# First attention of a four-layer kernel: where the rows of maxima are turned, and pairs of scores in the last waves

## The chip, the cores and the metric

The kernel runs as one program on one core of a Trainium2 chip. The metric is the device time of one execution in microseconds (us), as the median of several runs. The kernel before takes 2932.99 us in the median of 3 runs (2932.86 to 2940.77).

The engines are named as in the profile: PE (TensorE, matrix products and transposes), PEld (its weight loads), DVE (VectorE), ACT (ScalarE), POOL (GpSimd) and SP (the engine that issues the DMAs). PE writes its products into eight banks of PSUM (`P[:, 0]` to `P[:, 7]`), each 512 float32 wide on 128 partitions. Every engine runs its own list of instructions in order, and semaphores tie the lists together.

## What is computed

```python
x = L0_attn_x                                   # (4, 1024, 128)
x = x + attention(layernorm(x))                 # 16 heads of 8, inner layer norm, softmax, own residual
x = x + experts(layernorm(x))                   # a shared and 8 routed experts, top 2
x = x + differential_attention(layernorm(x))    # 8 heads, two softmaxes of 128 each
x = x + fp4_ffn(layernorm(x))                   # blockwise quantized
```

The change touches the first attention alone. For every batch and head it is

```python
scores = einsum('bhqd,bhkd->bhqk', q, k) / sqrt(8)
attn   = softmax(scores, axis=-1)
out    = einsum('bhqk,bhkd->bhqd', attn, v)
```

## The kernel before, in words

**Units and waves.** The first attention is cut into 16 units `u` (4 batches, 4 groups of four heads each). `plan_all` writes one order of steps by hand; each engine then walks through that order and takes the steps it has a part in. A stage `s` has 8 slots `i`. In every slot there is one `maxima` step of unit `u`, one `scores` step of a unit that lies `LAG0` = 7 stages back, and in slots 1 and 5 a `sums` step of one stage further back. What lies between two `sums` steps, four slots, is called a wave here. Unit `u` starts at stage `8u`.

**maxima (L1633 on PE, L1216 on DVE).** Queries times keys of one head `j` (32 of the array's rows) into one bank, 128x512; DVE reduces it to a row maximum. The four heads use four different row groups of the array. Banks: the ring 0, 1, 2, 3.

**row1, row2, row2_low.** When a unit has half of its maxima, `row1` (L1223, DVE) folds them into 16 columns, `row2` turns them with one PE transpose (L1639), ACT copies the result twice (L773, L774), POOL takes the rest (L2001), and SP issues eight small DMAs (L2097) that write the maxima into two rows of `a_Qs`. The `scores` of that half wait for these DMAs. The SP step also waits for all `maxima` that stand before it in the plan.

**scores (L1645 on PE, L780 on ACT).** Keys times queries of one head into one bank of the ring 5, 6, 7; ACT takes the exponential into `a_PT`. A wave has four of them.

**sums (L1660 on PE).** Probabilities times values, four heads in four column groups, 8 instructions, accumulated in bank 4. After eight of them ACT copies the bank to `a_OT` (L788).

**divide (L1668 on PE, L1230 and L1234 on DVE).** Four transposes of `a_OT`, then the division by the sums. Banks: the ring 0 to 3.

**Order around the change.** Slot 0: maxima of head 0, scores of head 2; slot 1: heads 1 and 3, then `sums`; slot 2: heads 2 and 0; slot 3: heads 3 and 1; slots 4 to 7 likewise. Further steps are hooked on behind a slot. `row2` of unit `u` stands behind slot 3 of stages `8u+4` and `8u+8`, and `divide` of unit `u-1` behind slot 4 of the same stages.

**The last waves.** From stage 128 on no maxima are left; the scores of unit 15 from its third wave on, and its sums, run with only the first steps of the experts beside them: statistics and normalization, `m_turn_x` (L1692), `route` (L1702, 24 small products), `choose`, `spread` (L1708), and `turn_o` (L1675) and `out_project` (L1683) of the last batch. After the last `sums` and the last `divide` the first expert item (L1721) starts.

Of the kernel before, what the change touches and what calls it, by code (L numbers as in the profile page):

```python
# [8 lines left out]
ACT = mybir.ActivationFunctionType  # L9
# [9 lines left out]
SCALE = float(8.0 ** -0.5)  # L19
NU = 4 * B  # L20
LAG0 = 7
NE, NI = 9, 256
LAG = 3
NITEM = 2 * B * 2 * NE
# [7 lines left out]

class Ctx:
    pass


class Once:
# [46 lines left out]
class Tally:  # L84
# [15 lines left out]
    def at(self, name, *step, i=None):  # L100

        return name, self.value[name, step] - (0 if i is None else self.by[name, step] - i)
# [44 lines left out]
def snapped(on_dve):  # L147
# [19 lines left out]
    "row2_low": lambda u, c: {"a_mt_low": 1, f"a_mdma{u % 3}_{c}": 128},  # L167
    "maxima": {"a_max_pe": 1, "a_max_dve": 1},
    "scores": {"a_st": 1, "a_exp": 1},
    "sums": lambda u, hs: {"a_pv": 1, "a_oe": 1} if hs % 8 == 7 else {"a_pv": 1},  # L170
    "divide": {"a_ot_pe": 1, "a_rc": 1, "a_on": 1},
    "turn_o": {"a_oc_pe": 1, "a_oc_act": 1},
# [69 lines left out]
    "row2": lambda *a: [("a_mt_act", "row2", *a)],  # L242
    "maxima": lambda *a: [("a_max_dve", "maxima", *a)],
    "scores": lambda *a: [("a_exp", "scores", *a)],
    "sums": lambda u, hs: [("a_oe", "sums", u, 15)],
    "divide": lambda *a: [("a_on", "divide", *a)],
    "turn_o": lambda *a: [("a_oc_act", "turn_o", *a)],
# [29 lines left out]
def plan_all():  # L277

    p = Plan()
    ring = Ring([0, 1, 2, 3])  # L280
    act_ring = Ring([5, 6, 7])

    def on_ring(*step):
        p.on([ring.take()], *step)

    def norm(who, b):
        return ([("ln_stats", who, b, k) for k in range(4)] + [("ln_gather", who, b, k) for k in range(2)] +
                [("ln_apply", who, b, k) for k in range(4)])

    def put(step):  # L290
        if step[0] in RINGED_ACT:
            p.on([act_ring.take()], *step)
        elif step[0] in RINGED:
            on_ring(*step)
        else:
            p.do(*step)
        for slots, s in FOLLOWS.get(step[0], lambda *a: ())(*step[1:]):
            p.later(slots, *s)
# [4 lines left out]
    def hook(s, slot, *step):  # L303
        hooks.setdefault((s + slot // 8, slot % 8), []).append(step)
# [14 lines left out]
    for u in range(NU):  # L319
        b, gr = divmod(u, 4)  # L320
        s0 = 8 * u
        if gr == 1 and b + 1 < B:
            for i, f in enumerate(norm("x", b + 1) + norm("xn", b + 1)):
                hook(s0, 5 * i + 4 * (i // 10), *f)
            for c in range(2):
                hook(s0 + 15 + c, 3, "turn_h", b + 1, c)
                hook(s0 + 19 + c, 7, "values", b + 1, c)
        if u + 1 < NU:
            for w, c in ((1, 0), (1, 1), (0, 0), (0, 1)):
                hook(s0 + 3 - w, 1, "project", u + 1, w, c)  # L330
        for c in range(2):
            hook(s0 + 3 + 4 * c, 7, "row1", u, c)
            hook(s0 + 4 + 4 * c, 3, "row2", u, c)
        e0 = s0 + LAG0
        for r in range(2):
            hook(e0 + 5 + 4 * r, 4, "divide", u, r)
            if gr == 3:
                hook(e0 + 6 + 4 * r, 7, "turn_o", b, r)
                hook(e0 + 7 + 4 * r, 5, "out_project", b, r)
# [14 lines left out]
    ahead = iter(ahead)  # L354
    for s in range(8 * NU + LAG0 + 2):
        for i in range(8):
            um, m = divmod(2 * s + i // 4, 16)
            ue, m_e = divmod(2 * (s - LAG0) + i // 4, 16)
            up, m_p = divmod(2 * (s - LAG0 - 1) + i // 4, 16)
            if um < NU:  # L360
                t, half = (m % 4, m // 4) if um == 0 and m < 8 else (m // 2, m % 2)
                on_ring("maxima", um, t, i % 4, half)
            if 0 <= ue < NU:
                p.on([act_ring.take()], "scores", ue, m_e, (i + 2) % 4)
            if i % 4 == 1 and 0 <= up < NU:
                if m_p == 0:
                    p.on([4], "sums", up, m_p)
                else:
                    p.do("sums", up, m_p)
            for step in hooks.get((s, i), ()):  # L370
                put(step)
            if ue == NU - 1:
                for step in next(ahead, ()):
                    put(step)
            p.tick()
# [15 lines left out]
    for b in range(1, B):  # L391
        m = 36 * (b - 1)
# [5 lines left out]
    at = [30, 33, 44, 66, 69, 80, 102, 105]  # L398
# [59 lines left out]
    for j in range(NJ - 1):  # L458
        n = 16 * j + 28.5
        at = {NJ - 3: (0, 1, 1.5, 6, 8, 10, 12, 14, 14.5, 18, 19, 20),  # L460
              NJ - 2: (0, 1, 1.5, 5, 6, 6.5, 7, 7.5)}.get(j, (0, 1, 1.5, 6, 8, 10, 12, 14, 14.5, 19, 20, 32))
# [63 lines left out]
def memory(nc, io):  # L525

    m = Ctx()
    where, top = {}, 16512

    def put(name, shape, dt, offset):  # L530
        t = nc.alloc_sbuf_tensor_at(name, shape, dt, offset=offset)
        where[t.name] = name, shape, offset
        return t

    def sb(name, shape, dt=F32):
        nonlocal top
        t = put(name, shape, dt, top)
        top += (4 * math.prod(shape[1:]) + 31) // 32 * 32
        return t
# [41 lines left out]
    assert top >= A_EARLY + 16384, top  # L581
    m.Ks[0] = sb("a_Ks0", [128, T], F32R)
    m.Qs[0] = sb("a_Qs0", [128, T], F32R)
    m.PT = [[sb(f"a_PT{j}_{i}", [128, 512]) for i in range(4)] for j in range(4)]
    m.Vp = [sb(f"a_Vp{i}", [128, NT * 144 + 32]) for i in range(2)]
    m.tq = [sb(f"a_tq{i}", [128, 512]) for i in range(2)]
    m.th = [sb(f"a_th{i}", [128, 512]) for i in range(2)]
# [117 lines left out]

def a_free(v, *step):

    return [v.at("a_oe", "sums", NU - 1, 7), v.at("a_oe", "sums", NU - 1, 15), v.at("a_st", "scores", NU - 1, 15, 1),
            v.now("a_add", *step), v.now("a_rc", *step)]


def scalar_engine(e, w, v, m):
    at, P = v.at, m.P8

    def bank(*step):
        return P[:, v.plan.bank[step], :]
# [59 lines left out]
    def scores(u, hs, j):  # L776
        w.wait_ge(*at("a_st", "scores", u, hs, j))
        if 16 * u + hs > 3:
            w.wait_ge(*at("a_pv", "sums", *divmod(16 * u + hs - 4, 16)))
        e.activation(m.PT[j][hs % 4][:, :], bank("scores", u, hs, j), ACT.Exp, scale=SCALE).then_inc(m.S["a_exp"])  # L780

    def sums(u, hs):
        c, kt = divmod(hs, 8)
# [32 lines left out]
    def item(n):  # L816
        w.wait_ge(*at("b_gate", "item", n))
        if n > 2:
            w.wait_ge(*at("b_hf", "product", n - 3))
        for t in a_free(v, "item", 0):  # L820
            w.wait_ge(*t)
        e.activation(m.sg[n % 3][:, :], bank("item", n), ACT.Silu).then_inc(m.S["b_sg"])  # L822
# [178 lines left out]
    def l_gate(i):  # L1001
# [1 line left out]
        w.wait_ge(*at("d_h_pe", "d_turn_h", NJ - 2, 1))  # L1003
        tanh(bank("l_gate", i), i)

    parts = dict(first=first, first_hn=first_hn, turn_h=turn_h, project=project, row2=row2, scores=scores, sums=sums,
                 turn_o=turn_o, m_turn_x=m_turn_x, choose=choose, spread=spread, item=item, halves=halves, down=down,
                 small_exp=small_exp, small2=small2, fold=fold, c_turn_x=c_turn_x, keep_x=keep_x,
                 c_project=c_project, exponent=exponent, turn=turn, pv=pv, output=output, weigh=weigh,
# [576 lines left out]
def tensor_engine(e, w, v, m):  # L1586
    at, P, ident = v.at, m.P8, m.ident

    def bank(*step):

        for t in v.freed(*step):
            w.wait_ge(*t)
        return P[:, v.plan.bank[step], :]
# [47 lines left out]
    def scores(u, hs, j):  # L1641
# [3 lines left out]
        e.matmul(ps, m.Ks[u % 3][r, 128 * kt:128 * kt + 128], m.Qs[u % 3][r, 512 * c:512 * c + 512],  # L1645
                 start=True, stop=True).then_inc(m.S["a_st"])

    def sums(u, hs):
        b, gr = divmod(u, 4)
        c, kt = divmod(hs, 8)  # L1650
        O = P[:, 4, :]
        for j in range(4):
            at_v = 144 * kt + 9 * (4 * gr + j)
            w.wait_ge(*at("a_exp", "scores", u, hs, j))
            w.wait_ge(*at("a_v_dve", "values", b, 1))
            if c:
                w.wait_ge(*at("a_oe", "sums", u, 7))
            elif u:
                w.wait_ge(*at("a_oe", "sums", u - 1, 15))
            tt = e.matmul(O[32 * j:32 * j + 32, :], m.Vp[b % 2][:, at_v:at_v + 32], m.PT[j][hs % 4][:, :],  # L1660
                          start=(kt == 0), stop=(kt == 7))
        tt.then_inc(m.S["a_pv"])

# [241 lines left out]
    def l_down(i):  # L1905
# [1 line left out]
        w.wait_ge(*at("d_hT", "d_turn_h", NJ - 1, i))  # L1907
        down_rows(ps[:, 0:128], i).then_inc(m.S["d_dn"])

    parts = dict(turn_h=turn_h, values=values, project=project, maxima=maxima, row2=row2, scores=scores, sums=sums,  # L1910
                 divide=divide, turn_o=turn_o, out_project=out_project, m_turn_x=m_turn_x, route=route, spread=spread,
                 item=item, down=down, finish=finish, small2=small2, fold=fold, c_turn_x=c_turn_x,
                 c_project=c_project, score=score, turn=turn, pv=pv, output=output, turn_weights=turn_weights,
# [272 lines left out]
def build(nc, io, out):  # L2186
    with ExitStack() as ctx:
        v = Tally(plan_all(), SIGNALS, READ)
        m = memory(nc, io)
        m.P8 = ctx.enter_context(nc.psum_tensor("P", [128, 8, 512], F32))  # L2190
        names = ["id", "mh", "a_w", "b_w", *[f"x{b}" for b in range(B + 1)], *v.end]
        m.S = {n: ctx.enter_context(nc.semaphore(n)) for n in dict.fromkeys(names)}
        block = ctx.enter_context(nc.Block())
        block.sync(lambda e: sync_engine(e, Once(e, m.S), v, m, io, out))
        block.scalar(lambda e: scalar_engine(e, Once(e, m.S), v, m))
        block.vector(lambda e: vector_engine(e, Once(e, m.S), v, m))
        block.gpsimd(lambda e: gpsimd_engine(e, Once(e, m.S), v, m))
        block.tensor(lambda e: tensor_engine(e, Once(e, m.S), v, m))
# [66 lines left out]
```

## Time and profile before

| | |
|---|---|
| median of 3 runs | 2932.99 us |
| profiled execution, its own time | 2927.33 us |
| its span | 2925.5 us |
| PE busy | 2744.2 us (94%) |
| DVE busy | 2307.5 us (79%) |
| ACT busy | 2100.6 us (72%) |
| POOL busy | 1802.3 us (62%) |
| first attention in full waves (73.28 to 805.31 us) | 240 waves |
| its last 16 sums without maxima | 805.31 to 861.8 us |

The profiled execution is one run; 1.8 us of its time lie outside the span. Busy shares are means over stages that have different limits, so the stages are read one by one. A matmul of 0.49 us that starts at the same time as its neighbours runs beside them in another row group: the starts tell the pace, not the durations. PEclk is the TensorE clock that the chip granted: 1.00 is 2.4 GHz, 0.50 is 1.2 GHz. A time in square brackets is idle time of the engine ahead of an instruction, with what ended it.

### The profile page before, as it was taken

What the parts mean: (1) busy time and instruction counts of PE and PEld (TensorE: products, weight loads), DVE (VectorE), ACT (ScalarE), POOL (GpSimd) and SP (SyncE); (2) the same over time, 40 slices, a digit from 0 to 9 for tenths busy, and PEclk for the clock granted to TensorE, in tenths of its full rate; (3) what the DMA queues carried; (4) which work ended last, traced back from release to release, by engine and by line L of the source; (5) the groups of instructions that cost most, each with busy time, mean ns of one, the idle gap of its engine ahead of it and who ended that gap; (6) DMA issues with size and microseconds to landing.
All of it is one profiled execution on the core that took longest, in us unless ns stands there. A gap on an engine that the chain in (4) does not pass through costs nothing.

```text
span 2925.5 us, 46589 instructions
## 1 busy us (share of the span) xinstructions
PE 2744.2 (94%) x16447; PEld 2037.2 (70%) x16447; DVE 2307.5 (79%) x4143; ACT 2100.6 (72%) x4692; POOL 1802.3 (62%) x1357
## 2 busy tenths in 40 slices
PE   6999999999899999999999999999999999999996
PEld 3333333333347777788888888888888888888885
DVE  8888888888937887778788777788777877777776
ACT  2777777777755555677777777777777777787773
POOL 3432534332115555677788778788778787777873
PEclk9999999999979999999999999999999999999997
DMA  1000000000021121000000000000000000000000
GB/s 41 7 7 7 12 7 7 7 7 2 2 76 53 47 73 59 8 1 1 1 1 3 1 3 3 3 1 3 3 1 3 3 1 3 3 1 3 3 3 6
DMA packets 25689, 34.83 MB, mean 12 GB/s; under 512 B 4136, under 2 KB 14952, under 8 KB 25456
## 3 DMA queue, kind: packets, MB, share of 16 engines
q1 hardware_dynamic: 25456, 31.85, 3.5%
q8 instruction: 131, 2.15, 0.3%
q14 instruction: 102, 0.84, 0.1%
HBM read 29.08 MB, written 2.23 MB: 11 GB/s over the span
## 4 chain that ended last, share of the span: by engine, by line
PE 69%; DVE 10%; ACT 10%; POOL 5%; issue 5%; DMA 0%; DVEq 0%; POOLq 0%
PE P L1792 17%; PE P L1817 11%; PE P L1660 9%; PE P L1645 5%; PE P L1721 5%; PE P L1803 5%; PE P L1633 4%; ACT a_PT L780 4%; PE P L1826 3%; PE P L1732 3%; PE P L1775 2%; PE P L1623 2%; DVE c_nm L1371 2%; ACT c_P L904 2%; POOL d_tn L1094 2%
## 5 line engine op out<-in xcount | busy, mean ns | idle before, releaser
L1371 DVE TENSOR_REDUCE c_nm<-P 128x1 f32<-128x1024 f32 x512 | 623.8, 1218 | 169.3 <-PE P L1792 169.1
L1216 DVE TENSOR_REDUCE a_mx<-P 128x1 f32<-128x512 f32 x1024 | 640.1, 683 | 94.9 <-PE P L1633 91.6
L904 ACT ACTIVATE c_P<-P,c_nm 128x1024 f32<-128x1024 f32 x512 | 576.0, 1125 | 131.6 <-DVE c_nm L1371 131.4
L780 ACT ACTIVATE a_PT<-P 128x512 f32<-128x512 f32 x1024 | 537.2, 602 | 165.5 <-PE P L1645 165.1
L2039 POOL TENSOR_TENSOR c_P<-c_P,c_P 128x1024 f32<-128x1024 f32 (+1 forms) x256 | 623.2, 2434 | 21.4
L2037 POOL TENSOR_SCALAR c_P<-c_P,c_rr 128x1024 f32<-128x1024 f32 (+1 forms) x256 | 304.4, 1189 | 305.0 <-DVE c_rr L1383 304.9
L1792 PE MATMUL P<-c_xth,c_Th 128*128 128x512 f32 x1024 | 365.8, 438 | 42.8 <-ACT c_P L904 42.6
L1645 PE MATMUL P<-a_Qs,a_Ks 32*128 32x512 f32 x1024 | 343.0, 491 | 59.1 <-ACT a_PT L780 52.6
L1817 PE MATMUL P<-c_DT,c_xkh 128*128 128x256 f32 x2048 | 392.0, 284 | 5.6 <-DVE c_xkl L1363 5.0
L1396 DVE TENSOR_TENSOR c_DT<-P,c_DT 128x512 fp32r<-128x512 f32 x512 | 348.6, 681 | 12.9 <-ACT c_DT L915 12.1
L1817 PEld LDWEIGHTS P<-c_DT,c_xkh 128*128 128x128 f32 x2048 | 330.1, 192 | 6.6 <-DVE c_xkl L1363 5.6
L1792 PE MATMUL P<-c_xtl,c_Th 128*128 128x512 f32 x1024 | 321.4, 395 | 0.0
L1792 PE MATMUL P<-c_xth,c_Tl 128*128 128x512 f32 x1024 | 321.2, 395 | 0.0
L1803 PE MATMUL P<-ident,c_P 128*128 128x128 f32 x2048 | 306.8, 272 | 6.6 <-DVE c_DT L1396 6.5
L915 ACT ACTIVATE c_DT<-P 128x512 fp32r<-128x512 f32 x512 | 309.8, 605 | 1.0 <-PE P L1803 1.0
L1633 PEld LDWEIGHTS P<-a_Ks,a_Qs 32*128 32x128 f32 x1024 | 128.1, 189 | 247.8 <-DVE a_mx L1216 192.1
L2025 POOL TENSOR_TENSOR b_sg<-b_sg,b_cwB 128x512 f32<-128x512 f32 x128 | 176.5, 1382 | 196.8 <-ACT b_sg L822 196.8
L1633 PE MATMUL P<-a_Ks,a_Qs 32*128 32x512 f32 x1024 | 284.2, 494 | 11.3 <-DVE a_Qs L1208 5.4
L1817 PE MATMUL P<-c_DT,c_xkl 128*128 128x256 f32 x1024 | 290.6, 284 | 0.0
L1660 PE MATMUL P<-a_PT,a_Vp 128*32 128x512 f32 x2048 | 280.8, 621 | 0.0
L1803 PEld LDWEIGHTS P<-ident,c_P 128*128 128x128 f32 x2048 | 245.2, 140 | 28.6 <-DVE c_DT L1396 8.0
L1645 PEld LDWEIGHTS P<-a_Qs,a_Ks 32*128 32x128 f32 x1024 | 133.9, 186 | 167.2 <-ACT a_PT L780 141.9
(245 smaller groups left out, 5418.4 us busy)
## 6 DMA issues: line engine op xcount, KB each, us to landing
b_cwB<-cw_scratch SPq DMA_DIRECT2D x64, 256.0 KB, 5.1
c_stg<-in_cw SPq DMA_DIRECT2D x8, 640.0 KB, 3.9
a_Qs<-a_mT SPq DMA_DIRECT2D x256, 2.0 KB
b_stg<-in_moe SPq DMA_DIRECT2D x9, 384.0 KB, 3.1
out<-xres SPq DMA_DIRECT2D x15, 128.0 KB, 1.8
xres<-in_x SPq DMA_DIRECT2D x3, 512.0 KB, 7.2
xres<-in_x SPq DMA_DIRECT2D x2, 256.0 KB, 3.1
a_hTl_f<-in_wqk SPq DMA_DIRECT2D x1, 512.0 KB, 3.7
```

Of the source, the lines that this page charges most:

```text
L780: e.activation(m.PT[j][hs % 4][:, :], bank("scores", u, hs, j), ACT.Exp, scale=SCALE).then_inc(m.S["a_exp"])
L904: e.activation(m.P1[s][n % 4][:, :], P[:, k:k + 2, :].rearrange("p c k -> p (c k)"), ACT.Exp, bias=m.nm[:, n % 4, s:s + 1], accum_out=m.sm ...
L1216: e.tensor_reduce(m.mx2[u % 2][:, t // 4, j, t % 4, half:half + 1], bank("maxima", u, t, j, half), AX, ALU.max).then_inc(m.S["a_max_dve"])
L1371: e.tensor_reduce(m.nm[:, n % 4, s:s + 1], P[:, k:k + 2, :].rearrange("p c k -> p (c k)"), AX, ALU.max, negate=True).then_inc(m.S["c_nm"])
L1396: e.tensor_tensor(lo, bank("turn", n, half).rearrange("p (t q) -> p t q", t=4), hi.bitcast(F32), ALU.subtract).then_inc(m.S["c_dl"])
L1633: e.matmul(ps, m.Qs[u % 3][r, 128 * t:128 * t + 128], m.Ks[u % 3][r, 512 * half:512 * half + 512], start=True, stop=True).then_inc(m.S["a_ ...
L1645: e.matmul(ps, m.Ks[u % 3][r, 128 * kt:128 * kt + 128], m.Qs[u % 3][r, 512 * c:512 * c + 512], start=True, stop=True).then_inc(m.S["a_st"])
L1660: tt = e.matmul(O[32 * j:32 * j + 32, :], m.Vp[b % 2][:, at_v:at_v + 32], m.PT[j][hs % 4][:, :], start=(kt == 0), stop=(kt == 7))
L1792: tt = e.matmul(ps[:, c, :], a[:, s, qs], x[:, 512 * c:512 * c + 512], start=(i == 0), stop=(i == 2))
L1803: tt = e.transpose(ps[:, 128 * i:128 * i + 128], m.P1[0][n % 4][:, 128 * kt:128 * kt + 128], ident)
L1817: tt = e.matmul(ps[:, 0:256], x[:, 128 * kt:128 * kt + 128], m.DT[p % 2][l][:, kt, :], start=(kt == 0 and j == 0), stop=(kt, j) == (7, 2))
L2039: e.tensor_tensor(p0, p0, p1, ALU.add).then_inc(m.S["c_D"])
```

## The change

Two things are moved or added, both in the first attention.

1. `row2` is hooked behind slot 5 instead of slot 3 of the same stage. In slot 5 it stands right behind the `sums`. Its followers (`row2_low`, two slots later) move with it.
2. The scores of the last unit from stage 128 on (`hs` 2 to 15) become `pair` steps: two matmuls into two neighbouring banks, (2, 3) for heads 2 and 3 and (5, 6) for heads 0 and 1, with one semaphore increment, and one exponential over both banks (128x1024). For that `a_PT` becomes one tensor. The other steps of that stretch have the rings 0, 1 and 7.

```diff
+SCORE_HEADS = ((2, 3), (0, 1))
+def paired(u, hs):
+    return u == NU - 1 and hs >= 16 - 2 * LAG0
+def scores_of(u, hs, j):
+    return ("pair", u, hs, 1 if j < 2 else 0) if paired(u, hs) else ("scores", u, hs, j)
...
+    score_pairs = Ring([(2, 3), (5, 6)])
...
-            hook(s0 + 4 + 4 * c, 3, "row2", u, c)
+            hook(s0 + 4 + 4 * c, 5, "row2", u, c)
...
+            if um == NU and m == 0 and i == 0:
+                ring.slots, ring.i, act_ring.slots, act_ring.i = [0, 1], 0, [7], 0
+            if 0 <= ue < NU and paired(ue, m_e):
+                if i % 2 == 0:
+                    p.on(score_pairs.take(), "pair", ue, m_e, i % 4 // 2)
+            elif 0 <= ue < NU:
                 p.on([act_ring.take()], "scores", ue, m_e, (i + 2) % 4)
...
-    m.PT = [[sb(f"a_PT{j}_{i}", [128, 512]) for i in range(4)] for j in range(4)]
+    m.PT = sb("a_PT", [128, 4, 4, 512])
...
+    def pair(u, hs, k):                                   # ACT
+        first, j = v.plan.bank["pair", u, hs, k], SCORE_HEADS[k][0]
+        w.wait_ge(*at("a_st", "pair", u, hs, k))
+        w.wait_ge(*at("a_pv", "sums", *divmod(16 * u + hs - 4, 16)))
+        e.activation(m.PT[:, j:j + 2, hs % 4, :], P[:, first:first + 2, :], ACT.Exp, scale=SCALE).then_inc(m.S["a_exp"])
...
+    def pair(u, hs, k):                                   # PE
+        c, kt = divmod(hs, 8)
+        bank("pair", u, hs, k)
+        first = v.plan.bank["pair", u, hs, k]
+        w.wait_ge(*at(f"a_mdma{u % 3}_{c}", "row2_low", u, c))
+        for i, j in enumerate(SCORE_HEADS[k]):
+            r = slice(32 * j, 32 * j + 32)
+            tt = e.matmul(P[:, first + i, :], m.Ks[u % 3][r, 128 * kt:128 * kt + 128],
+                          m.Qs[u % 3][r, 512 * c:512 * c + 512], start=True, stop=True)
+        tt.then_inc(m.S["a_st"])
```

## Rows read from the trace of the kernel before

**Rows 1.** Chain of waits, two waves; columns: start us, us, what.
```profile
412.53 0.99 PE P L1660 x8
413.52 0.42 PE P L1633
...
414.01 0.61 ACT a_PT L780
...
414.66 0.50 PE P L1645
...
420.01 0.50 PE P L1645
420.50 0.59 PE P L1668 x4
```

**Rows 2.** Timeline of PE, the wave with row2 and divide; start us, us, instruction.
```profile
417.79 1.07 PE L1660 MATMUL P<-a_PT,a_Vp 128*32 128x512 f32 x8
...
419.23 0.28 PE L1639 MATMUL P<-ident,a_nm 128*16 128x128 f32 x1
419.43 0.50 PE L1633 MATMUL P<-a_Ks,a_Qs 32*128 32x512 f32 x1
...
421.44 1.06 PE L1660 MATMUL P<-a_PT,a_Vp 128*32 128x512 f32 x8
```

**Rows 3.** Groups of PE's instructions by line, 100 to 800 us.
```profile
L1639 PE MATMUL P<-ident,a_nm 128*16 128x128 f32 x29 | 8.0, 277 | 0.4
```

**Rows 4.** Timeline of PE, a wave with the projection of the values between its groups.
```profile
195.69 1.07 PE L1660 MATMUL P<-a_PT,a_Vp 128*32 128x512 f32 x8
...
197.13 1.16 PE L1612 MATMUL P<-a_wv,a_hT 128*128 128x128 f32 x8
...
198.65 1.07 PE L1660 MATMUL P<-a_PT,a_Vp 128*32 128x512 f32 x8
```

**Rows 5.** Timeline of DVE, over the same two waves as rows 2.
```profile
418.05 3.16 DVE L1216 TENSOR_REDUCE a_mx<-P 128x1 f32<-128x512 f32 x5
...
422.97 2.48 DVE L1216 TENSOR_REDUCE a_mx<-P 128x1 f32<-128x512 f32 x4 [0.66 <-PE P L1633]
```

**Rows 6.** Timeline of SP's queue: the eight small DMAs behind row2.
```profile
421.28 4.88 SPq L2097 DMA_DIRECT2D a_Qs<-a_mT  x8
```

**Rows 7.** Busy time by stretch of the last waves; the value behind POOL's is PEclk.
```profile
815.00:845.00 30.00, 28.37 (x105) 11.86 (x106) 5.42 (x19) 14.31 (x29) 0.00 (x0) 0.50 0.00 1
845.00:862.00 17.00, 15.61 (x92) 5.69 (x91) 1.24 (x3) 12.03 (x25) 0.00 (x0) 0.98 0.41 127
```

**Rows 8.** Timeline of PE, last waves: a plain one at half clock, one at full.
```profile
838.10 1.94 PE L1660 MATMUL P<-a_PT,a_Vp 128*32 128x512 f32 x8
...
841.44 0.79 PE L1645 MATMUL P<-a_Qs,a_Ks 32*128 32x512 f32 x1 [0.68 <-ACT a_PT L780]
842.16 1.94 PE L1660 MATMUL P<-a_PT,a_Vp 128*32 128x512 f32 x8
...
848.73 1.07 PE L1660 MATMUL P<-a_PT,a_Vp 128*32 128x512 f32 x8
...
851.33 1.07 PE L1660 MATMUL P<-a_PT,a_Vp 128*32 128x512 f32 x8
```

**Rows 9.** Timeline of ACT: four exponentials in a row, and one of 1024 columns.
```profile
411.38 2.06 ACT L780 ACTIVATE a_PT<-P 128x512 f32<-128x512 f32 x4 [0.57 <-PE P L1645]
...
1598.93 1.11 ACT L904 ACTIVATE c_P<-P,c_nm 128x1024 f32<-128x1024 f32 x1 [2.27 <-DVE c_nm L1371]
1599.94 0.19 ACT L904 ACTIVATION_READ_ACCUMULATOR c_P<-P,c_nm 128x1 f32 x1
```

**Rows 10.** Timeline of DVE, the end of the maxima.
```profile
805.44 1.27 DVE L1216 TENSOR_REDUCE a_mx<-P 128x1 f32<-128x512 f32 x2
```

**Rows 11.** Timeline of PE, third wave without maxima, and the last sums.
```profile
809.63 1.93 PE L1660 MATMUL P<-a_PT,a_Vp 128*32 128x512 f32 x8
...
859.53 2.30 PE L1660 MATMUL P<-a_PT,a_Vp 128*32 128x512 f32 x16
```

More of the change, by code:

```diff
@@ L169 @@
     "scores": {"a_st": 1, "a_exp": 1},
+    "pair": {"a_st": 1, "a_exp": 1},
     "sums": lambda u, hs: {"a_pv": 1, "a_oe": 1} if hs % 8 == 7 else {"a_pv": 1},
@@ L244 @@
     "scores": lambda *a: [("a_exp", "scores", *a)],
+    "pair": lambda *a: [("a_exp", "pair", *a)],
     "sums": lambda u, hs: [("a_oe", "sums", u, 15)],
@@ L362, in plan_all @@
                 on_ring("maxima", um, t, i % 4, half)
-            if 0 <= ue < NU:
+            if um == NU and m == 0 and i == 0:
[4 more added lines that the diff above has]
+            elif 0 <= ue < NU:
                 p.on([act_ring.take()], "scores", ue, m_e, (i + 2) % 4)
@@ L706, in a_free @@
 def a_free(v, *step):
-    return [v.at("a_oe", "sums", NU - 1, 7), v.at("a_oe", "sums", NU - 1, 15), v.at("a_st", "scores", NU - 1, 15, 1),
+    return [v.at("a_oe", "sums", NU - 1, 7), v.at("a_oe", "sums", NU - 1, 15), v.at("a_st", "pair", NU - 1, 15, 1),
             v.now("a_add", *step), v.now("a_rc", *step)]
@@ L779, in scores @@
             w.wait_ge(*at("a_pv", "sums", *divmod(16 * u + hs - 4, 16)))
-        e.activation(m.PT[j][hs % 4][:, :], bank("scores", u, hs, j), ACT.Exp, scale=SCALE).then_inc(m.S["a_exp"])
+        e.activation(m.PT[:, j, hs % 4, :], bank("scores", u, hs, j), ACT.Exp, scale=SCALE).then_inc(m.S["a_exp"])
+    def pair(u, hs, k):
[3 more added lines that the diff above has]
+        e.activation(m.PT[:, j:j + 2, hs % 4, :], P[:, first:first + 2, :], ACT.Exp, scale=SCALE).then_inc(m.S["a_exp"])
     def sums(u, hs):
@@ L1004, in l_gate @@
         tanh(bank("l_gate", i), i)
-    parts = dict(first=first, first_hn=first_hn, turn_h=turn_h, project=project, row2=row2, scores=scores, sums=sums,
+    parts = dict(first=first, first_hn=first_hn, turn_h=turn_h, project=project, row2=row2, scores=scores, pair=pair, sums=sums,
                  turn_o=turn_o, m_turn_x=m_turn_x, choose=choose, spread=spread, item=item, halves=halves, down=down,
@@ L1653, in sums @@
             at_v = 144 * kt + 9 * (4 * gr + j)
-            w.wait_ge(*at("a_exp", "scores", u, hs, j))
+            w.wait_ge(*at("a_exp", *scores_of(u, hs, j)))
             w.wait_ge(*at("a_v_dve", "values", b, 1))
@@ L1659, in sums @@
                 w.wait_ge(*at("a_oe", "sums", u - 1, 15))
-            tt = e.matmul(O[32 * j:32 * j + 32, :], m.Vp[b % 2][:, at_v:at_v + 32], m.PT[j][hs % 4][:, :],
+            tt = e.matmul(O[32 * j:32 * j + 32, :], m.Vp[b % 2][:, at_v:at_v + 32], m.PT[:, j, hs % 4, :],
                           start=(kt == 0), stop=(kt == 7))
@@ L1908, in l_down @@
         down_rows(ps[:, 0:128], i).then_inc(m.S["d_dn"])
-    parts = dict(turn_h=turn_h, values=values, project=project, maxima=maxima, row2=row2, scores=scores, sums=sums,
+    parts = dict(turn_h=turn_h, values=values, project=project, maxima=maxima, row2=row2, scores=scores, pair=pair, sums=sums,
                  divide=divide, turn_o=turn_o, out_project=out_project, m_turn_x=m_turn_x, route=route, spread=spread,
```

## The prediction

> **What bounds the kernel now.** I read the chain of waits first, because PE is busy for 94% of the span and that alone does not say what a wave costs. In the steady part of the first attention the chain goes round a loop [rows 1]: sums (0.99), a first group of four matmuls in four row groups (0.42), the exponential of the first score (0.61), and only then the fourth score of the wave (0.50), whose bank that exponential frees, because four scores share three banks. With the small gaps that is a wave of 2.64 us. PE waits 0.28 in it and yet is the path.
>
> In the wave with both `row2` and `divide` the loop is longer [rows 1, 2]: sums to sums, 417.79 to 421.44, is 3.65 us. The turned rows take 0.20 of PE (419.23 to 419.43), and they take one of the three score banks, so that already the third score waits for the first exponential (to 420.01). The four transposes of `divide` (0.59) come only behind it, and the last pair of matmuls behind them. There are 29 such waves from 100 to 800 us [rows 3], all of 3.64 to 3.66 us, but three of 4.46 to 4.48 where transposes of the next batch's input stand in the same slot; the wave behind each takes 2.64 (2.95 in three).
>
> The last waves are another regime: no maxima, and a granted clock of 0.50 from 815 to 845 us [rows 7]. A plain wave takes 4.06 us there and 2.60 at full clock [rows 8], with PE waiting 0.68 for an exponential in the first.
>
> **Moving row2.** With `row2` gone from the wave, its third score finds a free bank and runs beside the third maximum. The wave is then sums 1.00, first group 0.43, second pair 0.43, `divide` 0.59, third pair 0.43: 2.88 us. The fourth score's bank is free by 1.21 us behind the start of the first group (0.56 to the exponential's start, 0.61, 0.04), and `divide` ends at 1.45, so nothing waits. A wave of the trace bears this way of reckoning out: with the projection of the values between its groups it gives 1.00 + 0.43 + 1.09 + 0.43 = 2.95, and the trace has 2.96 [rows 4].
>
> The next wave pays for the transpose behind its sums: 2.64 + 0.20 = 2.84. It takes a score bank there too, but the chain runs over the bank of the score behind it, and ACT's two copies fall into its idle 0.57 ahead of the exponentials [rows 9]. The transpose's price behind a burst of `sums` stands in no row; 0.20 is what it holds PE behind the row groups [rows 2], 0 and 0.5 (an exposed drain of its 0.28 on top) are the ends. Both waves: 3.65 + 2.64 = 6.29 before, 2.88 + 2.84 = 5.72 after, 0.57 less; 29 of them: **16.5 us**.
>
> What could eat it is DVE. Its work in the two waves is eight maxima at 0.62 (five take 3.16), 0.11 for `row1` and 0.5 for the division, 5.57 us [rows 5]. Before, it idled 0.66 in the second of the waves [rows 5]; after, 0.15 is left of 5.72. It fits, but in three stretches the statistics of the next batch stand on DVE too (0.3 us a wave). I take off 1 us for these: **15.5 us**, with 9 (a transpose at 0.4 and DVE late by some 0.02 a wave) and 17 as ends.
>
> The DMAs move as well. They are issued from 421.28 to 426.16 [rows 6], and the scores that need them start at about 434.7, six waves on. The step now comes two slots later (some 1.5 us) and the waves between are no longer; 4 us or more of slack stay. SP's wait for all earlier maxima grows by two of them; behind it on SP's queue are only loads of weights, needed much later. For the last half row (stage 128) the same chain lands some 3 us ahead of its scores.
>
> **The pairs.** First their start: the first pair wants banks 2 and 3, which the ring of maxima used last. By counting the ring's steps the very last of the maxima is in bank 2, and DVE ends it at 806.71 [rows 10]; the single score that stood here ran at 804.88. The first sums of the stretch (805.31) thus come 1.9 us later. This is regained within two waves: the third and fourth scores no longer wait for banks, and `row2`, which stood in PE's way there, comes behind them. I put the sums that began at 809.63 [rows 11] at about the same time.
>
> From there to the end of the last sums (859.53 + 2.30, so 861.8) it was 52.2 us [rows 11]. A plain wave after, at full clock: PE needs 1.00 + 0.43 if both pairs run together, 1.86 if not; ACT needs two exponentials of 1.01 each, the distance from a 1024-column exponential to what follows it [rows 9]. The second pair waits for the previous exponential of its bank pair, and the loop closes at about 2.1 us instead of 2.60. The gain is not from ACT: four single exponentials take 2.06 for a wave [rows 9], two wide ones 2.02. It comes from four banks in place of three.
>
> The Trainium skill ("ScalarE: Activation LUTs", "What ACT_TABLE_LOAD costs") gives an ACTIVATE with immediates 186 ns plus 0.833 ns a column, with 93 ns of overlap back to back. By it every pair would save ACT 93 ns, 2.6 us for the 28 pairs, where the rows show next to none.
>
> At half clock a plain wave is sums 1.86 and scores 0.72 on PE, 2.58 if both pairs run together and 3.16 when the second waits for ACT; these alternate, 2.87 in the mean, against 4.06 [rows 8]. Three cases follow for the 52.2 us:
> - Full clock throughout: four plain waves 8.5; six with transposes, copies or a division beside them at 2.55, 15.3; `spread` 2.3; the wave with both routings 7.05 (24 products at 0.21 are 5.2 of it, alike at either clock); `out_project` 2.95; the two last sums 2.2. In all 38.3, a gain of 13.9.
> - The old pattern, half clock from 815 to 845: the six waves in it come to 25.5 instead of 30.1; the full-clock waves around them save 0.5 each, some 3. Gain 7.5.
> - Half clock all along: about 51, gain 1.
>
> Which one? The clock fell at about 808 when the maxima ended, and stayed low while PE did scores in threes and ones, small routing products and waits; it held at full in the waves before, which were shorter, and from 845.5 on [rows 7]. After, scores come four at a time and PE's gaps halve, so I take the first case less 2 us for the half clock that the handover brings in any event: **12 us**, with 1 and 15 as ends.
>
> **Rivals.** (a) The clock behaves as before: 15.5 + 7.5 = 23, 2910 us. For it: the steps that stood in the stretch of low clock, transposes and the small routing products, all stay in it. (b) The clock stays low in the whole stretch: PE now idles some 2.6 us right before the first pair (from 804.1, when the last group of four matmuls with maxima ends, to 806.71), a gap that the trace before does not have. Then 15.5 + 1 = 16.5, 2916.5 us. The Trainium skill ("TensorE: Matmul & The Clock Gate", "What's actually happening") has it that the throttled state is the default and activity releases it, so that fewer matmuls in a loop may cost more than they save. That the clock fell behind the maxima agrees. (c) The move of `row2` gives nothing, because DVE, with 0.15 us to spare, takes the place of the bank wait: 12 us are left, 2921 us. Against it: DVE idles 0.66 there today. (d) Slower: the maxima rows land too late for their scores. PE would then stand before the first score of each half unit, on the semaphore of the eight DMAs, and everything behind it, maxima included, with it. It begins to cost once they land over 4 us later than now; 5.5 us later costs 1.5 a time, 45 us in 30 times, less the 28 gained: 2950 us. Nothing in the profile points there: the issue takes 4.88 us [rows 6] and its inputs move by 1.5. (e) More: full clock without a loss, 17 + 15 = 32, 2901 us.
>
> **The sum.** 15.5 + 12 = 27.5 us. Against the profiled execution's own 2927.33 that is 2899.8; it lies 5.7 under the median of the runs, whose lowest is 2932.86, so I forecast 2932.99 - 27.5 = 2905.5 us. The rest of the kernel only moves forward: the experts' weights are loaded long before, and the broadcast of the router's weights is issued six waves before its first use, 12.5 us after instead of 15.
>
> Chances: forecast 0.50, (a) 0.20, (b) 0.10, (c) 0.09, (d) 0.03, (e) 0.08. The range from 2898 to 2921 holds all but (d), half of (c) and some part of the uncertainty between runs. About 0.3% (8.8 us) is what a measurement can tell from no change: faster 0.93, same 0.04, slower 0.03.
>
> **What would show it.** The 29 waves with `divide` should be 2.88 and those behind them 2.84, with L1639 right behind L1660 at 0.20; DVE's idle time ahead of the sixth maximum should fall from 0.66 to about 0.1. The first pair should wait for DVE until about 1.9 us later than the score did. In the last waves ACT should go from one wide exponential into the next, waves of 2.1 us at clock 1.00, and the last sums should end some 12 us nearer to the first. Wrong would be: waves of `divide` still over 3.2 us (then the bank was not the reason), a second wave of 3.2 or more (DVE), or a PEclk of 0.50 over more than 10 us of the last waves (case a or b).

## The result, and the profile after

The changed kernel takes 2902.36 us in the median of 4 runs (2896.02 to 2903.36), the kernel before 2932.93 (4 runs, 2929.46 to 2940.77): 30.6 us less, a ratio of 0.9899 with a 95% interval of 0.9879 to 0.9919. The forecast was 2905.5.

The two profiled executions have spans of 2925.5 and 2901.2 us, 24.3 apart. Cut at landmarks of the traces, the difference is made of these parts:

| part | before | after | difference | forecast |
|---|---|---|---|---|
| start to the ninth sums | 100.96 | 104.72 | +3.8 | 0 |
| steady waves from there | 701.65 | 683.96 | -17.7 | -15.5 |
| the wave of the handover | 2.70 | 4.89 | +2.2 | +1.9 |
| from there to the end of the last sums | 56.5 | 39.7 | -16.8 | -13.9 |
| experts | 339.0 | 339.8 | +0.8 | 0 |
| second attention | 1665.3 | 1669.2 | +3.9 | 0 |
| rest | 59.4 | 58.9 | -0.5 | 0 |

**The page.** PE's busy row and the clock granted to it, in 40 slices:

```profile
PE   6999999999899999999999999999999999999996
PEclk6899999999999999999999999999999999999997
```

Ahead of the change the clock row had a 7 in its twelfth slice, the stretch of [rows 7]; here it is a 9. The 6 and the 8 in front are the half clock of the start, which this trace records. The trace before shows 1.00 there, although its matmuls had the pace of half clock up to about 80 us. So a PEclk of 1.00 ahead of the first recorded change of the clock (at 81.0 us in that trace) says nothing; the distance between matmuls does.

**The steady wave with the division, and the one behind it.** PE's timeline, to be laid beside [rows 2]:

```profile
414.41 1.07 PE L1696 MATMUL P<-a_PT,a_Vp 128*32 128x512 f32 x8
...
415.75 0.39 PE L1658 MATMUL P<-a_Ks,a_Qs 32*128 32x512 f32 x1
416.07 0.66 PE L1704 MATMUL P<-ident,a_OT 128*128 128x128 f32 x4
...
417.12 1.06 PE L1696 MATMUL P<-a_PT,a_Vp 128*32 128x512 f32 x8
418.12 0.28 PE L1664 MATMUL P<-ident,a_nm 128*16 128x128 f32 x1
418.32 0.50 PE L1658 MATMUL P<-a_Ks,a_Qs 32*128 32x512 f32 x1
...
419.97 1.07 PE L1696 MATMUL P<-a_PT,a_Vp 128*32 128x512 f32 x8
```

The wave takes 2.71 us (3.65 before) and the next 2.85 (2.64 before). The third score of the wave now runs with the first group, the division starts 0.66 behind that group, and the turned rows stand behind the sums and hold the next group by 0.20. The chain of waits no longer passes through an exponential in this wave:

```profile
416.14 0.59 PE P L1704 x4
...
417.19 0.99 PE P L1696 x8
418.18 0.21 PE P L1664
```

**DVE over the same waves** [rows 5]. Its idle time ahead of the sixth maximum is gone; what is left of it is the 0.16 ahead of the wave behind:

```profile
414.67 3.16 DVE L1241 TENSOR_REDUCE a_mx<-P 128x1 f32<-128x512 f32 x5
...
418.24 3.11 DVE L1241 TENSOR_REDUCE a_mx<-P 128x1 f32<-128x512 f32 x5
...
421.50 2.48 DVE L1241 TENSOR_REDUCE a_mx<-P 128x1 f32<-128x512 f32 x4 [0.16 <-PE P L1658]
```

Where the next batch's statistics stand beside a division, DVE has no idle time left, and it is what the wave (from 318.32, 3.27 us) waits for:

```profile
318.84 0.68 DVE L1241 TENSOR_REDUCE a_mx<-P 128x1 f32<-128x512 f32 x1
319.44 0.48 DVE L1183 BATCH_NORM_STATS2 ln_st<-xn 128x6 f32<-128x128 f32 x2
319.83 2.47 DVE L1241 TENSOR_REDUCE a_mx<-P 128x1 f32<-128x512 f32 x4
```

**The handover.** This is the wave from the last sums with maxima beside them to the first without. PE stands idle for 2.65 us ahead of the first pair (L1680), until DVE has reduced the last maximum (from 791.52, 1.27 long, so to 792.79), to compare with [rows 10]:

```profile
792.84 0.80 PE L1680 MATMUL P<-a_Qs,a_Ks 32*128 32x512 f32 x2 [2.65 <-DVE a_mx L1241]
793.57 1.94 PE L1696 MATMUL P<-a_PT,a_Vp 128*32 128x512 f32 x8
```

**The last waves.** First the stretches with PEclk (the value behind POOL's), then PE's waves at half and at full clock, which answer to [rows 7, 8], and ACT's exponentials in a row, which answer to [rows 9]:

```profile
793.00:800.00 7.00, 7.00 (x35) 1.98 (x39) 3.38 (x20) 3.49 (x6) 1.70 (x2) 0.55 0.00 1
800.00:812.00 12.00, 11.46 (x84) 5.72 (x80) 1.60 (x4) 10.55 (x12) 0.41 (x1) 1.00 0.01 3
812.00:820.00 8.00, 8.00 (x44) 2.33 (x48) 3.80 (x16) 5.36 (x7) 0.00 (x0) 0.57 0.00 0
820.00:834.00 14.00, 12.96 (x88) 4.21 (x87) 1.29 (x4) 11.10 (x14) 0.00 (x0) 1.00 0.43 143
```

```profile
813.62 1.93 PE L1696 MATMUL P<-a_PT,a_Vp 128*32 128x512 f32 x8
...
816.45 1.94 PE L1696 MATMUL P<-a_PT,a_Vp 128*32 128x512 f32 x8
...
822.02 1.07 PE L1696 MATMUL P<-a_PT,a_Vp 128*32 128x512 f32 x8
823.02 1.10 PE L1680 MATMUL P<-a_Qs,a_Ks 32*128 32x512 f32 x4
824.05 1.07 PE L1696 MATMUL P<-a_PT,a_Vp 128*32 128x512 f32 x8
```

```profile
822.55 4.06 ACT L805 ACTIVATE a_PT<-P 128x1024 f32<-128x1024 f32 x4
```

A plain wave is 2.03 us at full clock (2.60 before). The wave shown at half clock is 2.83 (4.06 before), but ACT has two small instructions of its own in it, at 815.55 and 815.70. A plain one at half clock is 2.60, as `pairs_only` has it from 831.85 to 834.44. ACT goes from one wide exponential into the next: four in 4.06 us, 1.01 apart, so at full clock ACT is now what a wave costs.

### The profile page after: what moved, and what is told of

Read it like the earlier page. It is cut to its first block, busy times and chain, and to the rows that moved or that the text cites. A ratio compares the mean times of both kernels' runs of the same rounds, so it can differ in the third digit from the quotient of the medians.

```text
span 2901.2 us, 46560 instructions
## 1 busy us (share of the span) xinstructions
PE 2730.1 (94%) x16447; PEld 2034.3 (70%) x16447; DVE 2304.3 (79%) x4143; ACT 2099.3 (72%) x4664; POOL 1800.3 (62%) x1357
## 4 chain that ended last, share of the span: by engine, by line
PE 67%; DVE 13%; ACT 10%; POOL 5%; issue 5%; DMA 0%; DVEq 0%; POOLq 0%; ACTq 0%
PE P L1828 17%; PE P L1853 11%; PE P L1696 8%; PE P L1839 5%; PE P L1757 5%; PE P L1658 4%; PE P L1670 4%; PE P L1862 3%; DVE a_mx L1241 3%; ACT a_PT L799 3%; PE P L1768 2%; PE P L1811 2%; PE P L1648 2%; DVE c_nm L1396 2%; ACT c_P L929 2%
## 5 line engine op out<-in xcount | busy, mean ns | idle before, releaser
L799 ACT ACTIVATE a_PT<-P 128x512 f32<-128x512 f32 x968 | 503.2, 605 | 112.2 <-PE P L1670 111.0
L1670 PE MATMUL P<-a_Qs,a_Ks 32*128 32x512 f32 x968 | 325.8, 487 | 42.7 <-ACT a_PT L799 36.4
L1828 PEld LDWEIGHTS P<-c_xth,c_Tl 128*128 128x128 f32 x1024 | 193.7, 189 | 45.7
```

The costliest lines, as they stand in the source:

```text
L799: e.activation(m.PT[:, j, hs % 4, :], bank("scores", u, hs, j), ACT.Exp, scale=SCALE).then_inc(m.S["a_exp"])
L1828: tt = e.matmul(ps[:, c, :], a[:, s, qs], x[:, 512 * c:512 * c + 512], start=(i == 0), stop=(i == 2))
```

## The experiments

All are laid beside the kernel before on the same chip; where a median is given, its ratio and interval are to that. Each group of experiments ran on another chip, so medians are compared within a group. Durations of waves are the distances from one burst of sums to the next on PE's timeline.

**One part alone: the rows moved.** The kernel before with

```diff
-            hook(s0 + 4 + 4 * c, 3, "row2", u, c)
+            hook(s0 + 4 + 4 * c, 5, "row2", u, c)
```

> Only row2 moved behind slot 5, the last waves as before. If the two parts are independent, the 29 waves with the division take 2.70 us and those behind them 2.85, 17.7 us less in the steady part, and the last waves take the old 56 us: about 2915 us in the median. If the pairs had given the whole gain by way of the clock, it would be 2930 or more. If the longer half clock at the start (to 94 us in the changed kernel, to about 80 before) comes from the moved row2, it is seen here too, and the gain is 14.

Median 2912.83 us against 2932.58, ratio 0.9923 (0.9891 to 0.9956): 19.8 us, with an interval from about 13 to 32, since its runs lie between 2898.92 and 2917.68. The waves are 2.70 and 2.84, the steady part takes 683.2 us, the handover 2.70, the last waves 54.3. The part stands by itself. The half clock of the start ended at 80 us here, so its 93 us in the first profile of the changed kernel was not the moved row's doing.

**The other part alone: the pairs.** The changed kernel with `row2` back in slot 3.

> Only the pairs and their banks, row2 back behind slot 3. Independent parts: the waves with the division take 3.65 again, the first pair waits some 2 us for the last maxima, and the last waves take about 40 us instead of 56.5: 14 to 15 us less than before, about 2918 us. If the clock in the last waves was luck, some 45 to 50 us for them and about 2925. The start should show full clock from 80 us on if the moved row2 is what kept it low.

Median 2922.9 us against 2932.58, ratio 0.9969 (0.9953 to 0.9986): 9.7 us (about 4 to 14), less than the 14 to 15 expected. The waves with the division are back at 3.65, the handover is 4.89, and the last waves take 41.9 us. The start had half clock up to 94 us with the rows in their old place, so the moved row does not cause it. Some 2 of the missing 4 to 5 us are in this kernel, whose last waves took 41.9 us and not 40. The others lie in what it is compared with: the last waves of the kernel before do not always take 56.5 us, as the next two show. Both parts together give 19.8 + 9.7 = 29.5; the changed kernel itself, in the same group, is 32.1 below the kernel before, well within the intervals.

**The two kernels again.** Each was run unchanged, `after_again` and `after_third` for the changed one, `before_again` and `before_third` for the one before.

> The changed kernel once more. It tells what repeats: 2.70 and 2.85 for the waves with the division and the transpose, 4.9 for the handover, about 40 us for the last waves. If the clock of the start and of the last waves depends on where the chip's own rhythm falls, the start stays at half to another moment than 94 us, by some us, and the median stays within 3 us of 2902.

> The changed kernel a third time, beside the next ones on the same chip. 2899 to 2903 us. The handover wave 4.9, last waves 39 to 40 us from the first sums without maxima to the end of the last ones.

> The kernel before once more, for its start and its last waves. If the end of the half clock at the start is the chip's own, it ends at another moment than 80 us; if it belongs to the order of the work, it ends there again. The half clock from 815 to 845 us should return, at most a few us shorter or longer.

> The kernel before a third time, for the clock in its last waves and at its start. The two looks so far had 34 and 14 us of half clock in the last waves, and these took 56.5 and 47.1 us. A third one should fall between 45 and 57 us, and the waves of the steady part should repeat to 0.02 us.

The changed kernel repeats: 2900.51 us (ratio 0.9881, 0.9858 to 0.9904) and 2900.63 (0.9892, 0.9877 to 0.9907), steady part 683.5 and 683.8, handover 4.9, last waves 39.0 both times. The kernel before repeats in its steady part (701.6), but its last waves took 47.9 us in one execution (not the 47.1 that the expectation of `before_third` names) and 56.6 in the other. The windows of the first:

```profile
807.00:830.00 23.00, 21.20 (x121) 9.25 (x121) 7.34 (x29) 15.44 (x31) 2.08 (x2) 0.90 0.01 2
830.00:842.00 12.00, 10.61 (x45) 3.25 (x42) 4.20 (x17) 7.77 (x17) 0.00 (x0) 0.62 0.00 0
```

and of the second:

```profile
809.00:826.00 17.00, 14.83 (x90) 5.66 (x90) 7.32 (x28) 14.13 (x29) 2.08 (x2) 1.00 0.01 1
826.00:866.00 40.00, 37.28 (x149) 13.75 (x148) 5.27 (x20) 19.02 (x37) 0.00 (x0) 0.53 0.17 54
```

The same program on the same data has 14 us of half clock here in one execution and 38 in the other. The last waves of all kernels together (half clock as the profile records it from the handover on):

| kernels | us of half clock -> us from the first sums without maxima to the end of the last |
|---|---|
| three banks, single exponentials | 34 -> 56.5, 14 -> 47.9, 38 -> 56.6, 31 -> 54.3, 17 -> 49.1 |
| pairs | 14 -> 39.7, 10 -> 39.0, 10 -> 39.0, 17 -> 41.9, 10 -> 39.7, 7 -> 38.7, 10 -> 39.1 |
| four banks, single exponentials (below) | 34 -> 48.8, 17 -> 43.2 |

At the same 14 us of half clock it is 47.9 against 39.7, so some 8 us belong to the change and not to the clock. At 17 us of half clock the table has all three: 49.1 with three banks, 43.2 with four and single exponentials, 41.9 with pairs. Of those 7.2 us the fourth bank has 5.9 and the pairs have 1.3. The split is rough: each of these is one execution, the half clock does not fall on the same waves in them, and the first and the third have `row2` in its old place.

**Was it the bank or the place?** The kernel before, `row2` still in slot 3, but in a bank of the maxima's ring:

```diff
-RINGED_ACT = {"turn_h", "project", "row2", "turn_o"}
+RINGED_ACT = {"turn_h", "project", "turn_o"}
```

> The kernel before, with row2 at its old place (behind slot 3) but in a bank of the ring of the maxima (0 to 3) in place of a score bank. If the price of the old place was the score bank, the wave with row2 and the division falls from 3.65 to 3.1 or 3.2 us (1.00 sums, 0.43, 0.20, 0.43, 0.59, 0.43, and up to 0.1 for the maxima's banks), and the one behind stays at 2.64. If the price was that the transpose breaks into the row groups, it stays at 3.5 to 3.65.

```profile
418.15 1.06 PE L1660 MATMUL P<-a_PT,a_Vp 128*32 128x512 f32 x8
...
419.58 0.28 PE L1639 MATMUL P<-ident,a_nm 128*16 128x128 f32 x1
...
419.79 0.50 PE L1645 MATMUL P<-a_Qs,a_Ks 32*128 32x512 f32 x1
420.42 0.66 PE L1668 MATMUL P<-ident,a_OT 128*128 128x128 f32 x4
...
421.44 1.07 PE L1660 MATMUL P<-a_PT,a_Vp 128*32 128x512 f32 x8
```

The third score follows the transpose at once (it came 0.58 behind the third maximum before), and the wave is 3.29 us: 0.36 of the old price was the score bank. The rest, 0.59 down to 2.70, goes with the place. The third pair starts 0.65 behind the first group (419.14 to 419.79) and not 0.34, of which 0.21 is the transpose. The division starts 0.63 behind that pair and not 0.32. About 0.2 of this is probably a wait for the bank of a maximum, since the ring has one more user; no run tests that. The wave is 3.29 to 3.31 in 18 of the 29; the eight in which DVE has other work take 3.59 to 3.87, and the three with transposes of the next batch's input 3.65. The steady part took 693.4 us, 8.3 less than before. Both explanations had a share, the place the larger one, and the expectation (3.1 or 3.2) was 0.1 too low.

**What does the transpose cost behind the sums?** The changed kernel with it done four times:

```diff
-        e.transpose(ps[0:16, 0:128], m.nm0[u % 2][c][:, :], ident).then_inc(m.S["a_mt_pe"])
+        for _ in range(4):
+            tt = e.transpose(ps[0:16, 0:128], m.nm0[u % 2][c][:, :], ident)
+        tt.then_inc(m.S["a_mt_pe"])
```

> The changed kernel with the transpose of row2 done four times in place of once. It measures what one transpose costs behind a burst of sums. If 0.20 us is its price on the path, of which some is a fixed part, the waves with it go from 2.85 to 3.2 or 3.3. If it hides behind the wait for an exponential there, they stay under 3.0.

```profile
418.12 1.06 PE L1698 MATMUL P<-a_PT,a_Vp 128*32 128x512 f32 x8
419.11 0.60 PE L1665 MATMUL P<-ident,a_nm 128*16 128x128 f32 x4
419.65 0.50 PE L1658 MATMUL P<-a_Ks,a_Qs 32*128 32x512 f32 x1
...
421.29 1.07 PE L1698 MATMUL P<-a_PT,a_Vp 128*32 128x512 f32 x8
```

The wave is 3.17 in place of 2.85: 0.11 for each further transpose, and 0.20 for the first. The transposes are on the path in full, and nothing hides them there.

**Four banks, or the wide exponential?** The changed kernel with single matmuls and exponentials in the last waves, over the same four banks:

```diff
-    score_pairs = Ring([(2, 3), (5, 6)])
+    score_pairs = Ring([2, 3, 5, 6])
...
-                if i % 2 == 0:
-                    p.on(score_pairs.take(), "pair", ue, m_e, i % 4 // 2)
+                p.on([score_pairs.take()], "scores", ue, m_e, (i + 2) % 4)
```

> The changed kernel, but in its last waves the four heads have one matmul, one bank (2, 3, 5, 6 in turn) and one exponential each, in place of pairs. If four banks in place of three are the gain, plain waves at full clock take 2.0 to 2.1 us as with pairs (2.03). If the wide exponential is, they take 2.4 to 2.6. The handover is then shorter, since the first score waits for one bank alone, not for two.

> Four banks and single exponentials in the last waves, once more and timed. The first look had half clock over nearly the whole stretch, with plain waves of 2.60 there, against 4.06 with three banks. If the low clock was where the chip's rhythm fell, it is shorter now and plain waves at full clock read 2.0 to 2.1; the median then lies within 3 us of the changed kernel's. If single exponentials keep the clock low, the stretch takes 48 us again and the median is 5 to 9 us above it.

The first execution fell into half clock for most of the stretch, and gave 48.8 us. Its plain wave there is 2.60, with all four matmuls together, which is what a plain wave with pairs takes at half clock:

```profile
827.87 1.94 PE L1695 MATMUL P<-a_PT,a_Vp 128*32 128x512 f32 x8
829.74 0.80 PE L1669 MATMUL P<-a_Qs,a_Ks 32*128 32x512 f32 x4
830.47 1.08 PE L1695 MATMUL P<-a_PT,a_Vp 128*32 128x512 f32 x4
```

The second has a plain wave at full clock:

```profile
821.04 1.06 PE L1695 MATMUL P<-a_PT,a_Vp 128*32 128x512 f32 x8
...
823.20 1.07 PE L1695 MATMUL P<-a_PT,a_Vp 128*32 128x512 f32 x8
```

That is 2.16, against 2.60 with three banks and 2.03 with pairs; the other plain wave, from 825.65, is 2.11 against 2.01. So most of the gain of a wave is the fourth bank, and 0.10 to 0.13 at full clock is the pairs'. The median is 2903.59 us (ratio 0.9907, 0.9892 to 0.9922), 3 above the changed kernel beside it, with overlapping intervals. The handover did not get shorter, although the first of the two expectations said that it would: it is 4.89 again. One bank alone, that of the last maximum, is enough to hold it.

**The handover, and DVE.** Two more. The first swaps the bank pairs, so that the first pair takes 5 and 6:

```diff
-    score_pairs = Ring([(2, 3), (5, 6)])
+    score_pairs = Ring([(5, 6), (2, 3)])
```

> The changed kernel with the two bank pairs swapped: the first pair in banks 5 and 6, the second in 2 and 3. If the 2.65 us that PE stands before the first pair come from the last maximum in bank 2, that wave falls from 4.9 to 3.1 or 3.2 us, held by the last exponential now; if something else holds it, it stays at 4.9. What follows is alike, so 1.7 us in all, too little to see in the median.

```profile
791.33 0.50 PE L1680 MATMUL P<-a_Qs,a_Ks 32*128 32x512 f32 x2 [0.85 <-ACT a_PT L799]
791.76 1.07 PE L1696 MATMUL P<-a_PT,a_Vp 128*32 128x512 f32 x8
```

The wait is 0.85 us, for the last single exponential, and the wave 2.79, less than the 3.1 to 3.2 expected. The second experiment adds another place for the next batch's statistics:

```diff
-            for i, f in enumerate(norm("x", b + 1) + norm("xn", b + 1)):
-                hook(s0, 5 * i + 4 * (i // 10), *f)
+            for at, f in zip((8, 13, 18, 23, 27, 29, 36, 41, 46, 51, 72, 77, 82, 87, 91, 93, 100, 105, 110, 115),
+                             norm("x", b + 1) + norm("xn", b + 1)):
+                hook(s0, at, *f)
```

> The changed kernel with the first pair in banks 5 and 6, and with the next batch's statistics (DVE) moved by 8 to 22 slots, so that none stands near a wave with the division. If DVE is what holds three of these waves at 3.27 us and two at 3.01, they fall to 2.70, some 2.3 us in all, and with the shorter handover (2.8 in place of 4.9, and about 1 us in the wave behind it) the median is some 5 us below the changed kernel's, about 2896. If something else holds these waves, they stay, and the gain is 3.

The three waves of 3.27 and the two of 3.01 are 2.70 now, which shows that DVE's statistics held them. But six others with a division, which now have a statistics step in the wave ahead of them, went from 2.70 to 3.00, as the one at 343.95 shows. The expectation of 2.70 for all of them failed:

```profile
342.68 0.37 DVE L1194 BATCH_NORM_AGGREGATE ln_mv<-ln_st 128x2 f32<-128x6 f32 x4
...
343.16 1.28 DVE L1242 TENSOR_REDUCE a_mx<-P 128x1 f32<-128x512 f32 x2
...
344.58 3.07 DVE L1242 TENSOR_REDUCE a_mx<-P 128x1 f32<-128x512 f32 x5
```

So of the 2.3 us hoped for, 0.6 came. It is likely that DVE, with some 0.15 us of idle time a wave, had not yet caught up with a step of 0.3 when the division came. The median is 2897.65 us (ratio 0.9883, 0.9869 to 0.9897), 3.0 below the changed kernel beside it, where 5 were expected. It is the lowest median of this study. The intervals overlap, and what tells the two apart is the handover in the trace, 2.93 us for 4.9.

## Why the prediction was right or wrong, point by point

**What bounds a wave** was read rightly in the direction and wrongly in the shares. `row_only` shows the whole gain of the steady part without the pairs. But the prediction named the score bank as the reason, and by its own terms the wave in another bank would be 3.08 (2.88 and 0.20 of transpose). `row_other_bank` has 3.29: the bank is 0.36 of the 0.95, and the place, with the transpose in the middle of the wave, 0.59. In the last waves `four_banks_again` bears the banks out, 2.16 for 2.60. That they bound the plain waves with maxima was read from the chain of waits [rows 1] and not tested.

**The wave with the division** was forecast at 2.88 and is 2.70. The term that was off is the second pair of matmuls, taken as 0.43 behind the first group; in the trace the division starts 0.66 behind the group, not 0.86, since the third maximum starts 0.34 behind the first group (415.75) and not 0.43. The trace before already had this, in a plain wave:

```profile
413.45 0.49 PE L1633 MATMUL P<-a_Ks,a_Qs 32*128 32x512 f32 x1
...
413.79 0.58 PE L1633 MATMUL P<-a_Ks,a_Qs 32*128 32x512 f32 x2
```

Probably the third pair uses row groups of the array that come free first; no run tests it. The check by the wave with the values could not show it, because there the values stand between the groups.

**The wave behind it**: 2.84 forecast, 2.85 measured, and the price of the transpose, 0.20, was right between its bounds of 0 and 0.5.

**DVE** was forecast to cost 1 us in three stretches. Three waves are 3.27 and two 3.01 in place of 2.70: 2.3 us, and PE waits for DVE in just these five. Three more are 3.03 (the first at 200.17). There DVE adds the bias of the values (L1222, 0.88 us) ahead of the maxima and has no idle time either, so another 1.0 us is probably its own; no run tests these. The sign and place were right, the size too small. Rival (c) was this effect over all 29 waves, and elsewhere its 0.15 us sufficed.

**The steady waves together** gave 17.7 us for 15.5. Against the 16.5 ahead of DVE's term, the 18 waves of 2.70 gave 3.2 more, the eight longer ones 1.9 less, and the rest 0.1 less (0.21 for the 0.20 of the transpose, and 3.65 for 4.47 in the three waves with transposes).

**The handover**: the wait for bank 2 was forecast to the tenth (2.65 us idle, 2.2 longer for 1.9). That it would be regained within two waves was wrong: it took four, and the clock was at half for the first 6.8 us of them. That is no accident of one execution. In all seven executions in which PE stood idle for 2.65 us ahead of the first pair, the clock fell within 1.5 us before that pair and stayed at half for 6.8 to 10.2 us. Of the three executions of the kernel before, which has no such wait, one had half clock there, for 3.4 us; of the two kernels with a first pair in banks 5 and 6, which wait only 0.86 us, one had 3.4 us and the other none. Rival (b) had named this gap; it brought 6.8 to 10.2 us of half clock, not a whole stretch of it.

**The DMAs** never held a score: in no run's trace does PE wait for one in the steady waves or the last ones. Rival (d) had no sign in any run.

**The last waves**: forecast 12 us with the handover. In the two profiles it is 16.8 - 2.2 = 14.6; but the profile of before was one with much half clock. Over its three executions the stretch took 53.7 us in the mean, after in its three 39.2, which makes 14.5 - 2.2 = 12.3. The plain waves were forecast well at full clock (2.1 for 2.03), less so at half (2.58 and 3.16 in turn, for 2.60 and 2.83). Two terms were off and made up for each other, which is luck. The routing wave was put at 7.05 on the claim that its small products take 0.21 each at either clock; they take 0.11 at full clock, and the wave 4.72 (and 24 times 0.21 is 5.0, not 5.2). The only rows I had of them were at half clock. And the clock: I took off 2 us for the half clock at the handover, and measured were 7 to 17 us of half clock in the stretch. The first profile had 13.7 us, so the prediction's own sign for case (a), over 10 us, was there, although the gain was that of the forecast.

A smaller slip: the clock did not stay at half from 808 on, as the prediction says; it was back at full from 811.4 to 814.8 and only then stayed at half to 845.6.

**The sum**: 17.7 + 12.3 = 30.0, beside a median 30.6 lower. Against the two profiled executions it is 24.3, because the second attention, which the change does not touch, took 3.9 us more and the start 3.8. The start does not repeat: its half clock ended anywhere from 80 to 95 us, and the ninth sums of the other two executions of the changed kernel began at 99.7 and 100.1. The second attention took from 1664.7 to 1672.8 us over all kernels, and 1665.0 and 1672.8 in two more executions of the kernel before; the changed kernel took 1669 in all three of its executions, which no run explains. The 0.8 us more of the experts do repeat, in every kernel with the new banks of the last waves, and their cause is open.

**Open.** Whether the pairs also keep the clock up: the three-bank kernels had 14 to 38 us of half clock in the last waves, the paired ones 7 to 17, four banks with single exponentials 34 and 17. The Trainium skill ("TensorE: Matmul & The Clock Gate", "What's actually happening") has it that activity releases the throttle. In the second execution shown above PE read as busy for 37.28 of 40 us while it was granted 0.53, so its busy row does not bear this out here. One to three profiles of each kernel, of a quantity that varies so much, do not settle it.

## What to carry to other kernels

When a small step shares a ring of PSUM banks with the step that sets the pace, its price is not its 0.2 us on PE alone. Here the wave with it was 0.95 us longer each time, 0.36 for the turn in the ring and 0.59 for its place between two groups of matmuls. Moved behind the sums it costs 0.21, so that 0.74 a time was given back. Before merging small instructions, count what is really gained: two exponentials in one saved ACT next to nothing, and the fourth bank that came with it did most of the work. Before an engine is left to wait for a bank, look at the clock behind the wait and not only at the wait. Where the granted clock differs between executions of one kernel, a single profile is a poor witness; lay several of the same kernel side by side before a difference is explained.

## What the runs showed of the hardware that was not expected

- The same program had 14, 34 and 38 us of half clock in the last waves of its first attention in three executions, and these took 47.9, 56.5 and 56.6 us. Its runs spread over 25 us (2920.53 to 2945.21), of which these waves explain some 9 at most; the second attention differed by 8 and the start by 4. The runs of the changed kernel spread over 8 (2896.02 to 2903.88), those of `row_only`, with three banks, over 19.
- Seven times out of seven the clock fell to half at the end of a wait of 2.65 us ahead of the first pair, and stayed there for 6.8 to 10.2 us.
- Small products of 128x8 are spaced 0.21 us at half clock and 0.11 at full.
- Four exponentials of 512 columns from PSUM take 2.06 us in a row, two of 1024 some 2.03. The 93 ns a pair that the figures of the Trainium skill ("ScalarE: Activation LUTs", "What ACT_TABLE_LOAD costs") gave are not seen.
- In a timeline the clock of the first 80 us can read 1.00 while the matmuls run at half their pace.
